# Unread identity products in TensorE's waits at the head of a gated delta-rule and expert kernel, with one shorter wait and one earlier rounding

## What is computed

```python
h = rms_norm(layernorm(x))                       # the head of the kernel: all 8 sequences
q, k, v = l2norm(silu(h @ Wq)), l2norm(silu(h @ Wk)), silu(h @ Wv)
beta = sigmoid(h @ Wb)
g = -exp(A_log) * softplus(h @ Wa + dt_bias)     # the decays: need h @ Wa of all tokens
alpha = exp(g)
# per token: S = alpha * S;  S += k outer (beta * (v - k.S));  o = q.S
gate = h @ Wg
x = x + (rms_norm(o) * o_norm_w * silu(gate)) @ Wo
y = square(relu(rms_norm(x) @ W_fc)) @ W_proj    # then the experts follow
```

## Time and profile before

| | |
|---|---|
| median of 3 runs | 2311.18 us (2311.15 to 2318.04) |
| the profiled execution, its own time | 2318.95 us |
| its span | 2317.2 us |
| PE busy | 2175.2 us (94%) |
| DVE busy | 1721.9 us (74%) |
| ACT busy | 1033.7 us (45%) |
| mean granted clock of TensorE | 0.984 |

### The profile page before, as it was taken

The page is one execution under the profiler, slowest core; times in us unless marked ns, Lnnn a source line. Parts: engine busy times, 40 slices in busy tenths (PEclk is TensorE's granted clock), DMA queues, the critical chain, the costliest instruction groups (busy, mean ns, idle before and its releaser), DMA issues. The chain is left out here.

```text
span 2317.2 us, 47223 instructions
## 1 busy us (share of the span) xinstructions
PE 2175.2 (94%) x16634; PEld 1939.2 (84%) x16634; DVE 1721.9 (74%) x4033; ACT 1033.7 (45%) x2152; POOL 674.6 (29%) x1030
## 2 busy tenths in 40 slices
PE   4769999999999999999999999888999999999998
PEld 4658888888888888888888888887899999999887
DVE  6568888888888888888888787477666666666653
ACT  2324444444444544444444443204455555545542
POOL 0113233232332332323322332000443434344332
PEclk9979999999999999999999999999999999999999
DMA  5321221222222222222221221001454454554331
GB/s 186 109 47 36 52 45 39 58 40 50 46 39 57 39 48 50 38 52 44 40 59 36 53 43 27 15 1 63 174 176 170 155 168 148 168 173 155 132 114 19
DMA packets 307902, 183.33 MB, mean 79 GB/s; under 512 B 244716, under 2 KB 286064, under 8 KB 298512
## 3 DMA queue, kind: packets, MB, share of 16 engines
q1 hardware_dynamic: 255184, 149.21, 22.6%
q0 software_dynamic: 11280, 29.31, 4.4%
q10 hardware_dynamic: 41264, 2.51, 1.1%
HBM read 150.23 MB, written 32.51 MB: 79 GB/s over the span
## 5 line engine op out<-in xcount | busy, mean ns | idle before, releaser
L650 DVE TENSOR_TENSOR w_lo<-w_raw,w_hi 128x512 fp32r<-128x512 f32 x288 | 190.4, 688 | 3.9
L790 PE MATMUL ps_back<-w_hi,eh_hi 128*128 128x256 f32 x624 | 180.1, 289 | 3.1 <-DVE eh_lo L660 3.1
L790 PE MATMUL ps_back<-w_lo,eh_hi 128*128 128x256 f32 x624 | 176.5, 283 | 0.0
L790 PE MATMUL ps_back<-w_hi,eh_lo 128*128 128x256 f32 x624 | 176.4, 283 | 0.0
L740 ACT ACTIVATE w_hi<-w_raw 128x512 fp32r<-128x512 f32 x288 | 169.5, 626 | 0.0
L752 ACT ACTIVATE sact<-ps_inva 128x512 f32<-128x512 f32 (+1 forms) x96 | 49.8, 519 | 236.7 <-PE ps_inva L790 213.3
L1305 ACT ACTIVATE v_s<-ps_front 128x512 f32<-128x512 f32 x64 | 38.0, 594 | 241.8 <-PE ps_front L790 241.8
L790 PE MATMUL ps_inva<-xT_hi,w_hi 128*128 128x512 f32 (+1 forms) x384 | 135.0, 352 | 2.1 <-DVE xT_lo L655 1.9
L1305 ACT ACTIVATE g_s<-ps_front 128x512 f32<-128x512 f32 x64 | 38.2, 597 | 217.7 <-PE ps_front L790 211.2
L790 PE MATMUL ps_inva<-xT_hi,w_lo 128*128 128x512 f32 (+1 forms) x384 | 134.8, 351 | 0.0
L790 PE MATMUL ps_inva<-xT_lo,w_hi 128*128 128x512 f32 (+1 forms) x384 | 134.8, 351 | 0.0
(11 more groups left out here) (410 smaller groups left out, 6585.0 us busy)
## 6 DMA issues: line engine op xcount, KB each, us to landing
w_raw<-L_ffn_W_gate_dram SPq DMA_DIRECT2D x24, 1024.0 KB
w_raw<-L_ffn_W_up_dram SPq DMA_DIRECT2D x24, 1024.0 KB
w_raw<-L_ffn_W_down_dram SPq DMA_DIRECT2D x24, 1024.0 KB
dT<-alphaT_d SPq DMA_DIRECT2D x32, 512.0 KB, 3.8
x_all<-L_attn_x_dram SPq DMA_DIRECT2D x4, 1024.0 KB, 10.0
hTr<-hT_d SPq DMA_DIRECT2D x32, 128.0 KB, 3.7
lt_d<-aP SPq DMA_DIRECT2D x256, 8.0 KB, 1.5
xi<-low_d SPq DMA_DIRECT2D x32, 128.0 KB
```

The lines of the kernel that those rows point to most:

```text
L650: V.tensor_tensor(piece(w_lo[p], m).bitcast(F32R), piece(w_raw, m), piece(w_hi[p], m), ALU.subtract).then_inc(split[n], 1)
L790: ins = MM(out_, w[a].bitcast(F32R), x[b].bitcast(F32R), start=start and n == 0, stop=stop and n == 2)
```

## The change

Identity products are put at eight places of TensorE's program: 100 at its very start, 10 and 36 after the transposes of sequences 0 and 1, 44 ahead of the first projection, 10 ahead of the decays' products, 34 ahead of the decays' transposes, 34 between the second and the third of the `delta_products`, and 6 behind each of the projections 4 to 7. The loop over the two halves of the first phase is written out. The decays' transposes wait for one link less of DVE's chain: for the exponent, no longer for the negated beta that follows it. ACT rounds `wproj` ahead of the value projections' evictions, and DVE takes the rest of it ahead of `lanes`.

```diff
@@ pe_decays
-            pe.wait_ge(dec_dve, ND_DEC)
+            keep_busy(psI[1][1], 34)
+            pe.wait_ge(dec_dve, ND_DEC - 1)
@@ ACT
             square_q(0)
+            act.wait_ge(tail_loaded, 16 * (3 + KD))
+            A(wproj_hi[:, :, :].bitcast(F32R), wproj, ACT.Copy).then_inc(vg_hi_ready, 1)
             for n in range(4, 8):
                 silu(0, n, True)
-            act.wait_ge(tail_loaded, 16 * (3 + KD))
-            A(wproj_hi[:, :, :].bitcast(F32R), wproj, ACT.Copy).then_inc(vg_hi_ready, 1)
@@ DVE
             q_sum(0, 0)
+            dve.wait_ge(vg_hi_ready, 4 * KD + 1)
+            V.tensor_tensor(wproj_lo[:, :, :].bitcast(F32R), wproj, wproj_hi[:, :, :], ALU.subtract).then_inc(vg_split, 1)
             lanes(0)
             decay_products(1)
-            dve.wait_ge(vg_hi_ready, 4 * KD + 1)
-            V.tensor_tensor(wproj_lo[:, :, :].bitcast(F32R), wproj, wproj_hi[:, :, :], ALU.subtract).then_inc(vg_split, 1)
@@ PE, first phase
             pe.wait_ge(consts, N_IDENT)
+            keep_busy(psF[0], 100)
             pe.wait_ge(small_loaded, 16 * 5)
...
-            with pe.Fori(0, BATCH // NB) as i:
+            for i in range(BATCH // NB):
                 for p in range(NB + 1):
                     if p < NB:
                         pre_transposes(NB * i + p, p)
+                        if i == 0 and p < 2:
+                            keep_busy(psF[0], (10, 36)[p])
@@ PE, chunk 0
+            keep_busy(psI[1][1], 44)
             pe.wait_ge(vg_split, 4 * KD)
             for n in range(4):
                 project(0, 0, n)
+            keep_busy(psI[1][1], 10)
             pe_decays(pe)
             transposes(0, FU_TK, k_s[:, 0])
             transposes(0, FU_TQ, q_s)
-            for n in range(4):
-                delta_products(0, n)
+            delta_products(0, 0), delta_products(0, 1)
+            keep_busy(psI[1][1], 34)
+            delta_products(0, 2), delta_products(0, 3)
             for n in range(4, 8):
                 project(0, 0, n)
+                keep_busy(psI[1][1], 6)
```

## The result

The median went from 2313.35 us (22 runs, 2307.86 to 2323.44) to 2322.15 us (22 runs, 2313.29 to 2329.76). The medians are 8.8 us apart. The ratio is 1.0029, 95% interval 1.0018 to 1.0041: slower by 4.2 to 9.5 us. The prediction said 2325.6 us, in 2309 to 2331. The profiled execution took 2326.11 us, span 2324.4, against 2318.95 and 2317.2 before. PE's busy time rose from 2175.2 to 2233.9 us and that of its weight loads (PEld) from 1939.2 to 2000.4; DVE, ACT and POOL stayed within 4 us.

A forecast was written before the change was run, and what follows sets the result against it. TensorE, busy 94% of the span, was taken to bound the kernel, so fills outlasting their waits delay the path. The third key product's +14.4 us, added to the median 2311.2, gave 2325.6 us, range 2309 to 2331.

The forecast's parts named there:

- The fills against their waits: TensorE's prologue: fills longer than their waits delay the path; of the 44's 12.3 us, 6.8 lie bare.
- The sum's instants: Start of sequence 0's small products; ends of first phase, 44, projections, ten; starts of decays' transposes, first, third key products.
- The price of a product: One identity product on TensorE is two records: 0.229 us at full clock, 0.44 us at half clock.
- The first 100: At TensorE's start: they end at 27.4 to 28.9 us, ahead of 29.12, so hidden.
- +14.4 forecast: Third key product in the prologue moves from 104.52 to 118.9 us, and the delay passes one for one into step 0.
- this mix never brought it up in 37 us: First phase: runs at 1.2 GHz throughout before; with the change full clock lasts 2.6 to 5.3 us, saving 2.9.
- rival A: Clock stays at 2.4 GHz through the whole first phase, ending at 63.1 us: -0.9 us, 2310; chance 0.14.
- B: First phase: clock lasts some 9 us, to the two small groups in a row, saving 6.7 us: 2322; chance 0.12.
- C: An identity product costs one record's 0.115 us, not two, if the pair overlaps: -3.2 us, 2308; chance 0.06.
- D: As rival A, and step 0's half-clock stretch runs at full clock too: -7.2 us, 2304; chance 0.05.
- E: Clock held in step 0 together with the main case: +8 us, 2319; chance 0.05.
- the costs at nothing: 6 products behind each of four projections (5.5 us in 12.79 idle), `wproj` rounding hidden in waits, written-out loop: nothing.

The follow-up runs named there:

- Experiments 5: The changed kernel without the 44 identity products ahead of the first projection; ratio to the kernel before 1.0013 (0.9998 to 1.0028).
- runs 6: The changed kernel without the 34 identity products between the second and third key products; ratio to the kernel before 1.0023 (1.0006 to 1.0041).
- 10: The changed kernel without the 34 identity products ahead of the decays' transposes; ratio to the kernel before 1.0002 (0.9990 to 1.0014).
- run 1: The kernel before with the shorter wait of the decays' transposes alone, no identity product; ratio 1.0000 (0.9983 to 1.0017).
- run 7: The kernel before with the earlier rounding of the projection weights alone; ratio 1.0000 (0.9985 to 1.0016).
- Run 9: The kernel before with fills sized to the waits, plus 4 and 14 products behind the transposes of sequences 0 and 1; 2304.46 us, ratio 0.9958.
- run 4: The kernel before with the first 100 identity products and 5 behind each of the eight small groups; ratio 1.0013 (0.9994 to 1.0031).
- 8: The kernel before with the first 100, 5 behind each small group, the shorter wait and fills sized to the waits; ratio 0.9991 (0.9975 to 1.0007).
- runs 2: The kernel before with the first 100 identity products alone; ratio 1.0012 (0.9997 to 1.0027).
- 11: The kernel before, unchanged, for a second trace; median of 12 runs 2311.11 us.

## Why the prediction was right, and where it was off

**The fills against their waits: right.** The sum's instants were 41.9, 76.2, 88.5, 94.1, 96.4, 105.3, 109.2 and 118.9 us. The trace has 41.8, 75.1, 87.2, 92.7, 95.0, 103.4, 107.0 and 116.4. The price of a product was 0.223 us (68 records in 7.59 us from start to start) against 0.229. Experiments 5, 6 and 10 put 4.9, 4.0 and 7.8 us on single fills. They add to 16.7 and not to 10.9 (41.3 less 30.4). The likely reason is that with one fill gone TensorE comes earlier, and more of the next one lies in a wait; no run takes two away. The first 100 were hidden as forecast: they ended at 28.2 us. Where the prediction counts 158 products between them and the third key product, there are 168: the ten behind the transposes of sequence 0 are left out. The sum itself has them.

**The size: +14.4 forecast, +11.9 between the two profiled executions, 8.8 between the medians.** The 2.5 us from 14.4 to 11.9 are small terms: 1.1 from the first phase, the rest from the L501 products (0.44 us apart at full clock and not 0.54), the fills, and the step from transposes to `alphaT` (0.85 us and not 1.16). The forecast time looks better than the forecast difference by luck: the median of 3 runs on which it stands was 2.2 us under that of 22, so it missed by 3.4 us where the difference missed by 5.6.

**The step that failed is "this mix never brought it up in 37 us", the clock in the first phase.** I read one execution as the program's behaviour, and the sum starts from its 74.1 us. With the same program ahead of it, the first phase of four traces (before twice, runs 1 and 7) ended at 74.1, 67.9, 74.2 and 71.1 us. That of the five with the change's first phase (the change twice, runs 5, 6 and 10) ended at 75.1, 73.0, 74.4, 72.4 and 72.2. In these five the clock held 3.6 to 6.3 us into the small products, where the sum has 2.6 to 5.3, and in runs 6 and 10 it came up once more, at 59 us, for 3.4 us. At half clock throughout, 37.2 us from the first small product on, these phases would end near 79 us. So the full clock saved 3.9 to 6.6 us where the sum takes 2.9. But before it saves something too: 0, 6.3, 0 and 3.1 us in its four traces, where the sum has nothing. On average the phase ends 1.6 us later; the sum has 2.1. The profile of before was a slow draw in another place too: from step 16's blocks to step 31's it took 629.4 us, and the other thirteen traces 625.9 to 628.2 us. Of the 4.7 us that the change seems to win back between the third key product and the end, 2.7 lie there; the other 2.0 are within the spread of the traces over that stretch (2204 to 2213 us).

**What stays open.** The traces give more than the medians: first phase 73.4 against 71.8 and behind it 41.3 against 30.4 are +12.5 us at the third key product, and from there to the end kernels with and without the change's first phase take 2208 us on average (five traces of each, 2204 to 2213). The medians are 8.8 apart, the ratio's interval is 4.2 to 9.5. In the changed kernel the time follows the mean granted clock of the run (correlation -0.93 over 22 runs: 2313.29 us at 0.985, 2329.76 at 0.978), and its two traces, of 2326.11 and 2322.49 us, are not near its lowest times. An estimate: 0.980 and 0.988 (2326.11 and 2313.57 us) are some 93 and 56 us at half clock, twice the missing share of the span, so the second execution has 37 us less of it. The profile has 34 us in a row at half clock from 46 us on. So in executions near 2313 us the clock may have held through the first phase, which is rival A, but no trace shows one. In the kernel before, time and mean clock hardly go together (correlation -0.04 to 0.23 in three sets of 29 to 31 runs); its mean counts the start of each run as full clock, whatever it was.

**Rivals.** A (the clock holds through the first phase) did not occur in any trace of the change; for its executions near 2313 us it is open. Run 9, with five products behind each small group, has what A describes. B's time was right to 0.2 us by chance: in the profile the clock held 4 us into the small products, not 9. C is out by the rows: 0.223 us a product. D and E did not occur in the traces: step 0 took 42.9 us in the change and 41.7 before. Of the costs at nothing, the rounding was nothing (run 7). The 6 behind each projection had no run of their own; in the trace of the change TensorE still waits 7.41 us behind them (12.79 before), so they lay in the wait.

## What to carry to other kernels

Price a fill by the record's pace in the same kernel and hold it against the wait as it will be once the earlier fills have moved the engine: 34 products of 0.223 us in a wait of 4 us are a delay, however warm they keep the array. Of the two kernels here that fill these waits and differ from before beyond noise, the one whose three places all kept a wait (run 9) was 9 us faster, and the one whose fills ran past their waits (the change) 9 us slower. A few dense products inside a thin phase held the clock up in three traces out of three (runs 4, 8 and 9) from 44 us on at the latest, but by themselves they gained nothing that the medians show. Where a path's speed hangs on the clock, one trace of before is one draw: take a second before adding anything to its median. My own -5.9 us of run 4 shrank to nothing against the second one.

## What the runs showed of the hardware

- A phase of transposes and 16-column float32 products ran at either clock level in one and the same program, without any gap in PE's work: it ended at 67.9 or at 74.1 us. In the five traces in which this mix, with nothing added behind its small groups, brought the clock up (runs 2, 6, 7, 10 and 11), the rise came within 0.6 us of the end of sixteen transposes in a row.
- Float32 transposes alone can stand ahead of a rise. In run 1 TensorE had waited 4.65 us and run nothing but transposes from 92.91 us on when the clock rose, at 96.9 us; in run 7 it had waited 5.79 us and run nothing but transposes from 91.22 us on when the clock rose, at 95.1 us.
- TensorE had run its transposes at full clock up to 33 us and was at half clock when a wait of 3.94 us ended (runs 4 and 8). With 14 products in that wait it was at full clock when the remaining 0.81 us ended (run 9).
- Sixteen small float32 records took 1.70 us at full clock and 3.27 us at half clock from the start of one group to the next, hardly less per record (0.106 us) than one of 128 columns (0.112 us).
- The granted clock reads 1.00 up to its first change in a trace. In the earlier trace rows the paces say half clock where the column would say 1.00, so ahead of the first change go by the paces. The mean granted clock of a run (0.984 before, 0.980 with the change) has the same fault and is no measure between two kernels.
